# Local blocks: probability transposes into free columns of the score banks, down projection into a projection bank, waits ahead of the masks; modulation and zeroing inside the first attention stage

## The reference

```
mod = silu(c) @ wmod            # six parts of 128: shift, scale, gate, twice
```

```
h = shift_tokens(x); q, k, v = split(h @ Wqkv)
q, k = rotary(l2norm(q) * qs), rotary(l2norm(k) * ks)     # heads of 64
sim  = q @ concat(previous window, this window of k).T * 8 ; masked
x    = x + softmax(sim) @ (same windows of v) @ Wo
h    = layernorm(shift_tokens(x)) * g + b
x    = x + (a * gelu(gate)) @ W2 + b2      where a, gate = split(h @ W1 + b1), 341 each
```

## Time and profile before

| | us |
|---|---|
| median of 3 runs (5280.88 to 5283.13) | 5283.05 |
| profiled execution, its own time | 5284.81 |
| its span | 5283.0 |
| PE, matmuls busy | 4702.6 (89%) |
| PE, weight loads | 3397.6 (64%) |
| DVE | 3876.1 (73%) |
| ACT | 3187.6 (60%) |
| POOL | 2745.1 (52%) |
| mean granted clock of PE | 0.956 |

### The profile page before, as it was taken

How to read it: one execution, slowest core, us unless ns; L and a number is a source line. 1 busy time by engine, 2 the same in 40 slices (tenths; PEclk the granted TensorE clock), 3 DMA queues, 4 the chain that set the end, 5 groups by cost and what they waited for, 6 DMA issues and landing times. The chain is left out here.

```text
span 5283.0 us, 215436 instructions
## 1 busy us (share of the span) xinstructions
PE 4702.6 (89%) x79056; PEld 3397.6 (64%) x79056; DVE 3876.1 (73%) x8260; ACT 3187.6 (60%) x6716; POOL 2745.1 (52%) x3885
## 2 busy tenths in 40 slices
PE   3568949999999999999999999999999576999996
PEld 2557736676767676776767676767676454666665
DVE  5984567777777777777777777777777566777775
ACT  1002526676767777667777677766776444777675
POOL 0004116666666666666666666666665325555552
PEclk6996969999999999999999999999999788999998
DMA  1000125455545454545454545455554003444442
GB/s 58 16 1 19 41 59 139 134 132 134 131 131 137 124 141 127 141 128 142 127 140 128 139 128 141 127 136 131 136 133 122 16 7 90 115 112 114 113 112 77
DMA packets 708752, 564.99 MB, mean 107 GB/s; under 512 B 227460, under 2 KB 633704, under 8 KB 707848
## 3 DMA queue, kind: packets, MB, share of 16 engines
q1 hardware_dynamic: 694920, 538.05, 38.4%
q10 hardware_dynamic: 13312, 22.02, 1.3%
HBM read 360.07 MB, written 200.02 MB: 106 GB/s over the span
## 5 line engine op out<-in xcount | busy, mean ns | idle before, releaser
L2128 POOL TENSOR_TENSOR L_qk<-L_cos_part,L_sin_part 128x512 f32<-128x512 f32 x896 | 1128.1, 1273 | 168.8 <-DVE L_sin_part L2013 168.6
L1798 ACT ACTIVATE L_squares<-L_ps_q 128x512 f32<-128x512 f32 x896 | 534.7, 597 | 964.9 <-PE L_ps_q L1539 958.7
L1539 PE MATMUL L_ps_q<-L_w_qkv,L_xT 128*128 128x512 f32 x1792 | 971.8, 625 | 20.9 <-DVE L_sin_part L2013 9.8
L2119 POOL TENSOR_TENSOR L_qk<-L_qk,L_rnorm 128x1024 f32<-128x1024 f32 (+1 forms) x512 | 864.2, 1688 | 20.3 <-POOL L_rnorm L2109 0.5
L1574 PEld LDWEIGHTS L_ps_t<-L_ident,L_qk 128*128 128x128 f32 x3584 | 445.4, 141 | 476.1 <-issue 372.8
L2012 DVE TENSOR_TENSOR L_cos_part<-L_ps_q,L_rot 128x512 f32<-128x512 f32 x896 | 610.4, 681 | 38.7 <-POOL L_rot L2138 34.4
L2013 DVE TENSOR_TENSOR L_sin_part<-L_ps_q,L_rot 128x512 f32<-128x512 f32 x896 | 610.1, 681 | 0.0
L2014 DVE TENSOR_REDUCE L_sumsq<-L_squares 128x8 f32<-128x512 f32 x896 | 605.7, 676 | 0.0
L2103 POOL TENSOR_TENSOR L_nw_a<-L_rnorm 128x32 f32<-128x32 f32 (+1 forms) x256 | 59.6, 233 | 1007.9 <-ACT L_rnorm L1828 1007.7
L1574 PE MATMUL L_ps_t<-L_ident,L_qk 128*128 128x128 f32 x3584 | 538.9, 273 | 3.1 <-DVE z L2076 2.1
L1809 ACT ACTIVATE L_qkT<-L_ps_t 128x512 f32<-128x512 f32 x896 | 530.5, 592 | 13.9 <-PE L_ps_t L1574 13.7
(11 more groups left out here) (289 smaller groups left out, 8977.7 us busy)
## 6 DMA issues: line engine op xcount, KB each, us to landing
L_val<-v_rows SPq DMA_DIRECT2D x896, 260.0 KB, 3.9
v_rows<-L_val SPq DMA_DIRECT2D x384, 260.0 KB, 2.1
v_rows<-L_val SPq DMA_DIRECT2D x512, 65.0 KB, 2.0
L_rot_base<-in_rot SPq DMA_DIRECT2D x256, 128.0 KB, 2.1
v_rows<-L_val SPq DMA_DIRECT2D x128, 130.0 KB, 2.1
L_x_in<-x_rows SPq DMA_DIRECT2D x512, 32.0 KB, 1.7
mid_rows<-z SPq DMA_DIRECT2D x256, 64.0 KB, 1.6
L_f_in<-mid_rows SPq DMA_DIRECT2D x256, 64.0 KB, 2.0
```

Source lines behind the costliest of these rows:

```text
L1539: nc.tensor.matmul(ps_q[j % 2][:, :], xT[:, parity(t), :], w_qkv[:, 0:2, 256 * j:256 * j + 256], start=True, stop=True).then_inc(S["proj_p ...
L1798: nc.scalar.activation(squares[:, j % 2, :], ps_q[j % 2][:, :], ACT.Square).then_inc(S["sq_done"], 1)
L2119: nc.gpsimd.tensor_tensor(v, v, r, ALU.mult).then_inc(S["normed"], 1)
L2128: nc.gpsimd.tensor_tensor(qk[:, t % 2, h, s, :], cos_part[:, j % 2, :], sin_part[:, j % 2, :], ALU.add).then_inc(S["added"], 1)
```

## The change

**Probability transposes.** They write P_VIEW, columns 256 to 512 of the two score banks. They no longer wait for the last copy of q and k and for their own copy before, but for shifted, DVE's last read of the scores. scores in turn waits for pT_done, the copy of the probabilities on ACT, before its masks; weighted_values drops that wait. In L1 out_transposes no longer waits for that copy. The up projection into the bank of the probabilities waits for the copy of q and k (L0) or of the output (L1) instead.

**Down projection.** In L0 it writes ps_q[0] and stands ahead of the feature transposes; the next but one projection waits for its reader new_done. ACT's affine and DVE's add_group lose their waits for each other.

**Waits ahead of the masks.** ready_to_project takes the waits that project had for xT_done, the weights and rotated, for the half that follows, and stands ahead of scores. scores takes its wait for qkT_done ahead of the masks, and its wait for the constants is gone.

**The front.** zero_rows and modulation_stage are gone; their loads, stores and steps stand in delta_attention_stage. wmod's buffer lies in state, sign and mag in prod. ACT brings out two of three parts in two instructions of 128 x 1024, DVE the third in four, behind group_stats. DVE waits for x alone, and takes the squares of k in two parts as k comes out.

```diff
@@ delta_attention_stage, sync @@
+                    for l in range(2):
+                        for b in range(2):
+                            sp.dma_start(c_in[:, 2 * l + b:2 * l + b + 1], c_rows[l][b, :].rearrange("(p o) -> p o", o=1)).then_inc(mod_in, 16)
+                        sp.dma_start(w_m[:, l, :], w_mod[l]).then_inc(mod_in, 16)
                     for b in range(2):
-                        sp.dma_start(xr[:, 16 * b:16 * b + 16, :], x_dram[b].rearrange("(t p) d -> p t d", p=128)).then_inc(loaded, 16)
+                        sp.dma_start(xr[:, 16 * b:16 * b + 16, :], x_dram[b].rearrange("(t p) d -> p t d", p=128)).then_inc(x_in, 16)
...
@@ vector @@
-                    dve.wait_ge(loaded, 144)
+                    dve.wait_ge(exped, 1)
...
+                    dve.wait_ge(x_in, 32)
                     group_stats(nc, dve, step, xr, mean, rstd, (st, mv, var, half, tmp))
+                    dve.wait_ge(mods_done, 2)
+                    raw = banks[:, :, 256:384]
+                    nc.vector.tensor_scalar(sign, raw, 0.0, 2.0, ALU.is_ge, ALU.mult).then_inc(mods_done, 1)
+                    nc.vector.tensor_scalar(mag, raw, -1.0, 0.25, ALU.mult, ALU.max).then_inc(mods_done, 1)
...
-                    dve.wait_ge(k_out, SUB)
...
                     for j in range(2):
+                        dve.wait_ge(k_out, SUB // 2 * (j + 1))
@@ local_block_stage @@
+        ps_d = ps_q[0][:, 0:256] if NS == 2 else ps_x[:, 256:512]
+        P_VIEW = ps_s[:, :, 256:512].rearrange("x b (i q) -> x b i q", i=2)
@@ tensor @@
+                def ready_to_project(k, T, hf):
+
+                    t, h = item(T, hf, AT_PROJ)
+                    if live(k, t):
+                        pe.wait_ge(S["xT_done"], tiles_(k, t))
+                        pe.wait_ge(wq_in[h], reloads(k, t, 16))
+                        wait(pe, S["rotated"], steps_(k, t, NS * h - 2))
+
                 def project(k, T, hf, s):
...
-                        pe.wait_ge(S["xT_done"], tiles_(k, t))
-                        if s == 0:
-                            pe.wait_ge(wq_in[h], reloads(k, t, 16))
-                        wait(pe, S["rotated"], steps_(k, t, j - 2))
+                        if s:
+                            wait(pe, S["rotated"], steps_(k, t, j - 2))
...
+                        if NS == 2 and j == 2 and parity(T) == TO_FT % 2:
+                            wait(pe, S["new_done"], groups_(k, T - TO_DOWN))
@@ prob_transposes @@
-                        if NS == 2:
-                            wait(pe, S["qkT_done"], steps_(k, t + 1, NS * h + NS - 1))
-                        else:
-                            wait(pe, S["oT_done"], halves(k, t, h - 1))
-                        wait(pe, S["pT_done"], halves(k, t, h - 1))
+                        read, g = item(T, hf, AT_SOFTMAX)
+                        if live(k, read):
+                            pe.wait_ge(S["shifted"], halves(k, read, g))
                         pe.wait_ge(S["exp_done"], halves(k, t, h))
@@ scores @@
-                        wait(pe, S["shifted"], halves(k, t, h - 1))
+                        v, g = item(T, hf, AT_PV)
+                        if live(k, v):
+                            pe.wait_ge(S["pT_done"], halves(k, v, g))
+                            wait(pe, S["att_done"], halves(k, v, g - 1))
+                        else:
+                            wait(pe, S["shifted"], halves(k, t, h - 1))
+                        pe.wait_ge(S["qkT_done"], steps_(k, t, NS * h + NS - 1))
                         wait(pe, S["kprev_done"], count(k, t, 1, 0))
                         for p in range(2):
                             nc.tensor.matmul(S_VIEW[:, p, :, :], ident_bf[:, :], masks[:, of_sequence(t), :].to_broadcast([128, HU, 2 * W]), start=True, stop=False)
-                        pe.wait_ge(consts_in, CONSTS)
-                        pe.wait_ge(S["qkT_done"], steps_(k, t, NS * h + NS - 1))
@@ weighted_values @@
-                        pe.wait_ge(S["pT_done"], mine)
-                        wait(pe, S["att_done"], before)
+                        s, _ = item(T, hf, AT_SCORE)
+                        if not live(k, s):
+                            pe.wait_ge(S["pT_done"], mine)
+                            wait(pe, S["att_done"], before)
@@ down_projection @@
-                        value_bank_read(k, T, 0)
+                        if NS == 2:
+                            t, h = item(T, 0, AT_PROJ)
+                            wait(pe, S["rotated"], steps_(k, t, NS * h))
+                            wait(pe, S["mid_done"], tiles_(k, T - TO_OUT - 1))
+                        else:
+                            value_bank_read(k, T, 0)
@@ emit @@
                     if goes_down and not early:
+                        down_projection(k, T)
                         feature_transposes(k, T)
-                        down_projection(k, T)
+                    ready_to_project(k, T + hf, 1 - hf)
                     scores(k, T, hf)
                     weighted_values(k, T, hf)
```

More of the change, by code:

```diff
@@ L103, in modulated_group @@
     nc.vector.tensor_tensor(out, out, vec(0), ALU.add).then_inc(done, 1)
[L106 to L155, removed]
-                        step(nc.vector.tensor_scalar(out[:, 1, :], src[:, 128:256], 1.0, None, ALU.add))
-                        step(nc.vector.tensor_scalar(sign[:, :], src[:, 256:384], 0.0, 2.0, ALU.is_ge, ALU.mult))
-                        step(nc.vector.tensor_scalar(mag[:, :], src[:, 256:384], -1.0, 0.25, ALU.mult, ALU.max))
-                        step(nc.vector.scalar_tensor_tensor(mag[:, :], src[:, 256:384], 0.25, mag[:, :], ALU.max, ALU.max))
-                        step(nc.vector.scalar_tensor_tensor(out[:, 2, :], sign[:, :], -1.0, mag[:, :], ALU.add, ALU.mult))
@@ L235, in _ @@
                 def _(pe):
-                    pe.wait_ge(loaded, 144)
+                    pe.wait_ge(mod_in, 96)
+                    pe.wait_ge(wide_done, 1)
+                    for k in range(4):
+                        for j in range(2):
+                            last = nc.tensor.matmul(ps[2 * k + j][:, 0:384], wide[:, k, :], w_m[:, k // 2, 384 * j:384 * j + 384], start=True, stop=True)
+                    last.then_inc(product, 1)
+                    pe.wait_ge(loaded, 112)
+                    pe.wait_ge(mods_done, 6)
                     for g in range(8):
@@ L1564, in qk_transposes @@
                         elif NS == 2:
-                            wait(pe, S["pT_done"], halves(k, t - 1, h - 1))
+                            wait(pe, S["qkT_done"], steps_(k, t, j - 1))
                             if hf == 1 and parity(T) == TO_UP % 2:
@@ L1587, in out_transposes @@
                         else:
-                            pe.wait_ge(S["pT_done"], halves(k, t, h))
+                            wait(pe, S["oT_done"], halves(k, t, h - 1))
                             if hf == 1 and parity(T) == TO_UP % 2:
@@ L1714, in up_projections @@
                         for made, which in [(("gate_ps", ((1, 0), (1, 1))), ("gate_ps", ((1, 2), (0, 2))), ("up_ps", ((0, 0), (0, 1))))[n] for n in parts]:
-                            if made == "up_ps":
-                                wait(pe, S["pT_done"], halves(k, item(T, 0, AT_PV)[0], item(T, 0, AT_PV)[1]))
+                            if made == "up_ps" and NS == 2:
+                                t, h = item(T, 0, AT_SCORE)
+                                wait(pe, S["qkT_done"], steps_(k, t, NS * h + NS - 1))
+                            elif made == "up_ps":
+                                t, h = item(T, 0, AT_OUT)
+                                wait(pe, S["oT_done"], halves(k, t, h))
                             for j, c in which:
```

64 lines of the change are left out of this document (39 added, 25 removed).

## The result

The change is slower: **5457.82 us** median of 4 runs (5453.52 to 5466.02) against 5282.99 (5280.88 to 5283.13), a ratio of 1.0333 with a 95% interval of 1.032 to 1.0345, or +175 us. The profiled execution took 5453.52, with a span of 5451.7.

What follows compares the result with a forecast made beforehand. PE's queue was taken to set the pace. L0 +91, L1 +88 and the front -32 sum to +147 us, a median of 5430 us, with a range of 5345 to 5510.

Steps and rivals of the forecast that it cites:

- Front, -32: Before L0: earlier loads of x start statistics and the first normalised group sooner (-27), squares of k partly covered (-4.6).
- Gain of the down half: L0's down half: 0.17 us from the dropped key-copy wait, 0.26 from val_done covered by the down projection, plus lighter projection waits.
- The up half gains nothing: L0's up half: whatever PE gains is waited away at the output transposes for att, so zero was counted.
- The loss in L0, "1.56 a cycle": Masks of L0's two halves 1 wait for ACT's copy of x, 0.78 us a half, 1.56 a cycle.
- 0.61: L0's whole gain in us a cycle, from waits dropped, covered by the down projection or moved off the projection.
- The 0.3 taken for the way from the copy to the masks: Time in us from the end of ACT's copy to PE's first mask, with 0 to 0.6 as bounds.
- the wait for xT costs 0.78: Each half 1 of L0: copy of x ends 0.48 us after the masks' old start, plus 0.3 to the first mask.
- L1, +88: L1: masks wait for the probability copy (down half, 1.10) or copy of x (halves 1, 1.28 and 0.37), 2.75 us a cycle.
- Rival 1: Waits ahead of the masks are met while earlier work runs, so the change is faster: 5192 us; chance 7%.
- Rival 2: Only the wait for the probabilities costs: L0 keeps -59, L1 loses 70, 5262 us; chance 4%.
- Rival 3: More gaps in L1 let PE's clock fall to 1.2 GHz, up to 6160 us; chance 2%.
- Rival 4: Each wait ahead of the masks costs 0.6 us, not 0.3: 5516 us; upper end of the main case, no separate chance.

Runs made afterwards that it cites:

- ready_only: The kernel before with ready_to_project ahead of scores alone, banks, down projection and front as before; 5489.46 us, ratio 1.0396.
- late_ready: The change with ready_to_project called from project again, so no wait for xT stands ahead of the masks; 5296.43 us, ratio 1.0026.
- front_only: The kernel before with the new front alone, the local stages as before; 5249.51 us, ratio 0.9936.
- act_order: The change with ready_to_project in project again, L1's probability transposes in their own bank, ACT normalising features behind its copy of x; 5167.79 us, ratio 0.9786.

## Why the prediction was right

The time, 5457.8 where 5430 stood, is inside the range, and each stage has its sign and nearly its size. The mechanism, waits for ACT's copies ahead of the masks, is the one that ready_only and late_ready show. But L0's size is partly luck: two sums that were both too small cancel, as the fourth point below has it.

- **Front, -32:** -32.4 in the trace and -32.4 in front_only. The statistics start at 14.5, not 16, and the first group at 35.7, not 37.
- **Gain of the down half:** 0.43 and 0.06 were predicted and 0.48 measured, by two errors that cancel. In late_ready this half takes 7.72, a gain of 0.68; the change loses 0.20 of it to the order of the waits ahead of the masks, and the prediction had no such loss.
- **The up half gains nothing:** -0.43 in the up half, and in the half behind it +0.39 from the output transposes' wait for att (1.89 us into the half, 1.50 before). Right, by the mechanism given.
- **The loss in L0, "1.56 a cycle":** right in place, too small in size, and matched by a gain that was too small as well. act_order has the shared banks and no late wait at the masks of L0's halves 1, and takes 3266.5: against it the change loses 184, or 1.92 a cycle where 1.56 stood, and the kernel before lies 81 above it, or 0.84 a cycle where 0.61 stood. The difference is 1.08, where 0.95 stood. (act_order also moves ACT's normalising; the kernel before had no late masks for that move to help.) The 0.3 taken for the way from the copy to the masks is 0.64 in the half 1 after a down half and 0.38 in the other. There the step "the wait for xT costs 0.78" names one of two waits: xT's comes last by 0.04 us, but without it the one for the probabilities holds the masks (late_ready), and taking xT's away gives back 0.26. The prediction asked where the copy of x ends in this half and not where the copy of the probabilities does, which stands on ACT behind the normalised features. The trace of the kernel before has it: that copy ended at 2531.00, 0.14 after the masks of the earlier trace rows had started, and the change makes the masks wait for it.

```profile
2530.42 0.58 ACT L1858 ACTIVATE L_probsT<-L_ps_t 128x512 f32<-128x512 f32 x1
```

- **L1, +88:** +95.7. The down half was to lose 1.10 and lost 1.14; the half 1 after an up half 1.28 against 1.66; the other 0.37 against 0.67, since here too the way to the masks is longer than 0.3; the up half gained 0.22, which I had as nothing. Sum 3.25 in the cycle shown and 2.99 over the stage, where 2.75 stood.
- **Rival 1** (waits hidden) fell; what is right in it is that waits which are met cost nothing when work lies in front of them, as ready_only's down half shows; where the copy is not yet made, in the halves 1, the masks waited. **Rival 2** (only the probabilities bite) is what late_ready shows of L1, +64 where it said 70, and in one half of L0 that wait is nearly as late as the one for xT; as the whole account it is out by 200 us. **Rival 3:** the clock stayed up, 1.00 in both stages. **Rival 4** (0.6 a wait) is near the truth in two of five places, 0.64 and 0.68; the others are 0.38, 0.44 and 0.35.

What stays open is 6 us: the median of the change's runs lies 4.3 above its profiled run, and the rest of the kernel after L1 took 1.9 longer, with nothing in that stage changed. In the twelve traces this rest takes from 45.1 to 50.9 us, so 1.9 is within what it varies by.

## What to carry to other kernels

A wait put earlier in an in-order queue is free only if the thing waited for is made before the queue gets there; look where its maker ends in every kind of iteration, not in one. When several waits stand at one point, put the one that is met last at the end, and remove them together: here one edit gave 57 us or none, depending on the wait beside it. When a queue is late for a reader, move the work that nobody waits for behind all its readers, and not just behind the first.

## What was not expected of the hardware

- Waits that are met still took PE's sequencer time when they stood behind one that was late, 0.09 to 0.16 us a row: the way from the end of ACT's copy to the masks was 0.64 us with the late wait first and 0.19 with it last, the same waits otherwise. With work in front of them the same waits cost nothing (6.54 us to the masks with and without).
- Order alone was worth 72 us of 5458, 1.3%, more than the whole new front.
